# Row gathers of a graph kernel: their indices copied four at a time, 24 tiles ahead, in place of halves of twelve

## The reference, cut to what matters

```
X      = einsum('ne,ref->rnf', out, weights[l])         # 9 edge types, 3 layers l
msg    = X[edge_type, src] + biases[l][edge_type]       # one row per edge
hidden = segment_sum(msg, dst)                          # relu between the layers
x      = layernorm(x + out)
...                                                     # then an attention over the same edges
x      = layernorm(x + attention(x))
```

## Time and profile before

| | |
|---|---|
| median of 3 runs | 4747.55 us (4741.61 to 4761.0) |
| the profiled execution | 4800.08 us, of which the span is 4798.3 us |
| PE busy, DVE busy, POOL busy | 3249.5 us (68%), 3108.2 us (65%), 2833.3 us (59%) |
| layer 0, from its first gather to its last sum | 616 to 1936 us |
| layer 1 | 1993 to 3117 us |
| layer 2, turns with cells | 3173 to 3626 us |
| layer 2, turns without | 3626 to 4257 us |
| attention and output | 4257 to 4798 us |

### The profile page before, as it was taken

How to read it: one execution, slowest core, us unless ns; L and a number is a source line. 1 busy time by engine, 2 the same in 40 slices (tenths; PEclk the granted TensorE clock), 3 DMA queues, 4 the chain that set the end, 5 groups by cost and what they waited for, 6 DMA issues and landing times.

```text
span 4798.3 us, 78742 instructions
## 1 busy us (share of the span) xinstructions
PE 3249.5 (68%) x13288; PEld 1889.5 (39%) x13289; DVE 3108.2 (65%) x9948; ACT 412.4 (9%) x713; POOL 2833.3 (59%) x2838
## 2 busy tenths in 40 slices
PE   7799745556555555766666666676665555669998
PEld 4333223334333333434444444444444444435333
DVE  9999865555555555666666666675664333356998
ACT  2000001000010000001010100101000000000332
POOL 0777866666656566277777777647777777720000
PEclk9899888877878888888889888897895555569998
DMA  5000014433343345645354363565344212134232
GB/s 156 20 0 0 0 45 71 64 58 62 58 65 69 58 61 60 159 67 81 68 76 72 70 78 66 72 155 81 67 65 88 53 53 53 52 54 144 107 133 81
DMA packets 391663, 341.02 MB, mean 71 GB/s; under 512 B 252658, under 2 KB 342314, under 8 KB 388104
## 3 DMA queue, kind: packets, MB, share of 16 engines
q0 software_dynamic: 90368, 165.49, 16.3%
q10 hardware_dynamic: 199392, 60.71, 13.0%
q1 hardware_dynamic: 101672, 112.75, 7.3%
HBM read 231.62 MB, written 107.13 MB: 71 GB/s over the span
## 4 chain that ended last, share of the span: by engine, by line
PE 30%; issue 21%; POOL 17%; DVE 15%; DVEq 9%; DMA 6%; ACT 2%; POOLq 0%; SPq 0%; ACTq 0%
PE ps L876 12%; POOL region L776 8%; POOL scattered_edges L758 8%; PE ps L867 6%; DVE region L510 5%; DVEq L270 5%; DMA region<-x_of_type,idx 5%; PE ps L928 4%; PE ps L910 3%; DVE region L451 3%; PE ps L936 3%; DVE oh L441 2%; PE ps L886 2%; DVEq L510 1%; DVEq L441 1%
## 5 line engine op out<-in xcount | busy, mean ns | idle before, releaser
L776 POOL DMA_INDIRECT region<-x_of_type,idx x2520 | 2435.4, 966 | 1202.3 <-issue 844.0
L876 PE MATMUL ps<-region 128*128 128x510 bf16 x4200 | 1488.7, 435 | 981.6 <-DVE region L451 805.8
L867 PE MATMUL ps<-oh,region 128*128 128x102 f32 x5040 | 1220.5, 334 | 458.4 <-DMA region<-x_of_type,idx 292.1
L867 PEld LDWEIGHTS ps<-oh,region 128*128 128x128 f32 x5040 | 1111.0, 240 | 1007.2 <-issue 333.0
L510 DVE TENSOR_TENSOR region<-region,ps 128x102 f32 x2520 | 657.9, 261 | 1159.3 <-PE ps L867 692.9
L876 PEld LDWEIGHTS ps<-region 128*128 128x128 bf16 x4200 | 451.9, 117 | 1177.9 <-issue 1152.1
L441 DVE TENSOR_SCALAR oh<-iota_w,arrays 128x102 f32<-128x102 f32 x2524 | 630.7, 294 | 162.1 <-issue 141.4
L450 DVE TENSOR_SCALAR region<-iota_w,arrays 128x640 bf16<-128x640 f32 x841 | 471.7, 561 | 221.9 <-PE ps L876 124.7
L758 POOL DMA_INDIRECT scattered_edges<-region x304 | 394.1, 1296 | 208.3 <-DVE ends L385 110.6
L846 PE MATMUL ps<-region 128*128 128x420 f16 x2016 | 410.3, 344 | 25.6 <-DVE region L415 25.6
L451 DVE TENSOR_SCALAR region<-iota_w,arrays 128x510 bf16<-128x510 f32 x841 | 416.7, 496 | 0.0
(11 more groups left out here) (176 smaller groups left out, 1527.8 us busy)
## 6 DMA issues: line engine op xcount, KB each, us to landing
region<-x_of_type,idx POOLq DMA_INDIRECT x2520
edge_counts<-region ACTq DMA_DIRECT2D x31, 1275.0 KB
region<-edge_counts SPq DMA_DIRECT2D x25, 1568.0 KB, 6.5
x_of_type<-region SPq DMA_DIRECT2D x50, 576.0 KB, 5.6
edge_absent<-region ACTq DMA_DIRECT2D x31, 637.5 KB
region<-edge_absent SPq DMA_DIRECT2D x25, 784.0 KB, 4.3
x_of_type<-x0st SPq DMA_DIRECT2D x51, 192.0 KB, 2.0
scattered_edges<-region POOLq DMA_INDIRECT x304
```

The source lines that it names most:

```text
L776: pool.indirect_dma_start(out=grow[:, u % GR, :], out_offset=None, in_=xt, in_offset=bass.IndirectOffsetOnAxis(ap=idx[:, u % GR:u % GR + 1 ...
L867: pe.matmul(ps[:, 6 + n % 2, t * RB:(t + 1) * RB], grow[:, u % GR, :], oh[:, u % U, 0:RB], start=True, stop=True).then_inc(s_used, 1)
L876: mm = pe.matmul(ps[:, c, 0:CW], cl[:, q % 2, c * P:(c + 1) * P], cr[:, q % 2, :], start=False, stop=False, skip_group_check=True)
```

## The change

`put_idx` copies four columns, those of the group of four tiles that has just been summed, and stands behind each of the six groups of the body. Ahead of the loops it is called six times in place of two. GpSimd waits for `s_idx` in front of each group of four and no longer for `s_used`: the copy comes behind the group's sums on VectorE, which come behind its matmuls.

```diff
-    HALVES = GR // 2
-    PUTS = {-(-HALVES * n // SLOTS) - 1: n + 1 for n in range(1, BODY // HALVES + 1)}
...
-            def put_idx(t, h):
-
-                nc_.tensor_copy(idx[:, h * HALVES:(h + 1) * HALVES],
-                                gix[:, bass.ds(t, HALVES)]).then_inc(s_idx, 1)
+            def put_idx(t, n):
+
+                nc_.tensor_copy(idx[:, n * SLOTS:(n + 1) * SLOTS], gix[:, bass.ds(t, SLOTS)]).then_inc(s_idx, 1)
...
-            put_idx(0, 0)
-            put_idx(HALVES, 1)
+            for n in range(GR // SLOTS):
+                put_idx(n * SLOTS, n)
...
-                    if n in PUTS:
-                        put_idx(i * BODY + PUTS[n] * HALVES, PUTS[n] % 2)
+                    put_idx(i * BODY + (GR + n * SLOTS), n)
...
                     for u in range(BODY):
-                        if u % HALVES == 0:
-                            reg_wait(pool, s_idx, i * (BODY // HALVES) + ((NT * l + u) // HALVES + 1))
                         if u % SLOTS == 0:
-                            reg_wait(pool, s_used, i * BODY + (NT * l + u + SLOTS))
+                            reg_wait(pool, s_idx, i * (BODY // SLOTS) + ((NT * l + u) // SLOTS + 1))
```

More of the change, by code:

```diff
@@ L78, in gnn_program @@
     assert CP <= REST and EP % U == 0 and U == 2 * KR and HW <= 512 and NT <= 1 << DIGIT
-    assert BODY == GR and GR % U == 0 and BODY % U == 0 and U == 2 * SLOTS and ET <= KW and NT // HALVES % 2 == 0
+    assert BODY == GR and GR % U == 0 and BODY % U == 0 and U == 2 * SLOTS and ET <= KW
     assert R * NP < 1 << ROW_BIT and RB <= P and ROW_BIT + 7 <= 2 * DIGIT and NB % JB == 0 and PAD_ROW <= NP
```

## The result

The kernel after takes 4819.26 us (4817.85 to 4823.78, 4 runs), the kernel before beside it 4752.32 us: a ratio of 1.0144, 95% interval 1.012 to 1.0168. The forecast was 4742 us with a range up to 4785. The profiled execution of after has a span of 4817.4 us, only 19 us more than that of before; the two medians differ by 67. Before's profile had also begun layer 0 late, at 616.6 us, where after's begins at 605.0 and the later profiles of the kernel before at 605 to 607; so the three layers by themselves have grown by 33 us. The experiments come back to that.

The account below looks back on a forecast made before the run. Layer 0 was taken as slowed by instruction fetches, layer 1 bound by VectorE and TensorE, layer 2's end by GpSimd. Terms 34 + 1 - 12 - 28 + 0 = -5 us on 4747.5 gave 4742 us, range 4700 to 4785.

Parts of the forecast that it names:

- Copies, +34 us: Layers 0 and 1: four more VectorE copies a turn cost 0.12 us each over 70 turns, +34 us; hidden in layer 2.
- The second rival: Layers 0 and 1, behind groups 0, 1, 3 and 4: copies cost 0.24 us each, +28 us, 4776 us; chance 0.20.
- the ring: Layers 0 and 1: TensorE waits for VectorE's L451, VectorE for TensorE's L867; a delay there was said to count once.
- GpSimd's waits, -12 us: Layer 2, turns with cells: GpSimd's waits for copies fall to the 0.30 us any gather shows, -12 us.
- Late gathers, -28 us: Layers 0 and 1: eight tiles more lead remove nearly all TensorE's waits for gathers delayed by ScalarE's stores, -28 us.
- The stall at the head, 0 between -17 and +17 us: Head of layer 0's turns: the body moves four places, still lies in four pieces, and the instruction-fetch stall stays; 0 us.
- an earlier start of the fetch at the turn's end: Layer 0's turns: roughly cancels the 0.3 us of four instructions moved behind the second fetch.
- The sum: Whole kernel: 34 + 1 - 12 - 28 + 0 = -5 us, giving 4742 us.
- I take the difference over as it is: The -5 us, worked out on a profiled execution of 4800.08 us, is applied unchanged to the runs' median of 4747.5 us.
- the copies are hidden: Rival: VectorE's waits before the sums take in the copies, leaving -39 us, 4708 us; chance 0.17.
- the deeper queue brings nothing: Rival: late gathers still stop TensorE and stops use up 24 tiles, +35 us, 4783 us; chance 0.06.
- The last rival: One more instruction ahead of the loop puts layer 0's body in three pieces, removing the stall: -200 - 5, 4542 us; chance 0.07.

Follow-up runs that it names:

- copies with the old waits at place 0: Kernel after with GpSimd's waits of before, layer 0's body at the start of a piece of 128 instructions: 4606.72 us, ratio 0.9612 to the kernel before.
- the kernel before at place 0: Kernel before with five tiny fills ahead of the first loop, so layer 0's body begins a piece of 128 instructions: 4587.91 us, ratio 0.9565 to the unchanged one.
- the ratios 1.0141 and 1.0048: Against the kernel before: kernel after with GpSimd's waits of before, 1.0141; kernel before with four tiny fills ahead of the first loop, 1.0048.
- place 127: Layer 0's body begins on the last place of its piece of 128 instructions: kernel before with four tiny fills, ratio 1.0048; kernel after unchanged, 1.0088.

## Why the prediction was wrong, point by point

**Copies, +34 us.** Size off, and dependent on what stands around them. The undisturbed turn of layer 1 grew by 0.4 us for four of them, near the 0.48 that was read. Without the stall the whole price is about 22 us (copies with the old waits at place 0, against the kernel before at place 0): 15 in layers 0 and 1, where 34 were put, and 5 in layer 2, where nothing was. What hides the rest was not tried. With the stall it is about 44 us by the ratios 1.0141 and 1.0048, of which the profiled stages show 25 in layer 0 and 7 in layer 1. The second rival (the copies cost double) came near for layer 0: 25 us on 34 turns of 4 copies are 0.18 us each, between the forecast 0.12 and its 0.24, and in two of the four places some 0.28. Its reason, a delay paid twice in the ring, was not shown.

**GpSimd's waits, -12 us.** Right: in after's profile all waits above 0.3 us are gone from layer 2 once it has begun, and the layer gained 13 to 18 us in every pair of kernels that differ in them. (The working puts GpSimd's busy share at 0.71 to 0.74 everywhere; in layer 0 it is 814.24 of 1320 us, 0.62. No term hangs on it.)

**Late gathers, -28 us.** The mechanism was right, the size only in part. No wait of TensorE for a gather is left after the first turns. Yet layers 0 and 1 gained 14 us by the new waits without the stall, and with it 8 in layer 1 and nothing in layer 0: there TensorE's waits for late gathers went from 14 us to none, and its waits for L448 rose from 473 to 492.

**The stall at the head, 0 between -17 and +17 us.** This is the step that failed: "an earlier start of the fetch at the turn's end" didn't come, and the four instructions behind the second fetch were not cancelled by anything. They were priced at 0.3 us, 10 us in 34 turns; the heads measured +16, and the end of the turn, where the gain was to be, +8. Alone the move measured +24 us by the ratio, +30 in the profiled stage. That the body would still lie in four pieces, and the counts of 171 and 2 packets, were right. Beside the stall the copies cost more than without it: by ratios 0.93% against 0.47%, and 0.48% for the place. This is a second step that failed: the sum adds the two terms as if neither hung on the other.

**The sum.** 24 for the place, 44 for the copies and -25 for the new waits make +43 us against -5; each is a difference of two ratios along one path from before to after, so the sum must come to the 44 that after showed. The other 23 us of the first comparison are not explained. "I take the difference over as it is" rests on a median of 4747.5 us that the experiments don't repeat: beside them this kernel took 4776 to 4808 us in every run on four chips, near the first profile's 4800. The 4752 us are 0.8% below those chips, and after's 4819 only 0.3% below its 4836; why is open, since no profile of the kernel before at 4752 us was taken.

**The other rivals.** That the copies are hidden (4708 us) and that the deeper queue brings nothing (4783 us) are both ruled out: copies alone cost 22 us without the stall and 44 with it, and the queue alone gained 45 and 25. **The last rival** (chance 0.07) was right in mechanism and price and missed by one instruction: -208 us for the kernel before, where it had -200.

## What to carry to other kernels

Before pricing an edit inside a hardware loop, count instructions: where a body reached into a fourth piece of 128 instructions, as here, each turn paid for fetches, and one to five dummy instructions ahead of the loop were worth ten times the edit that was being discussed (208 us against 21). Measure an edit at a fixed place of the body, or its own effect drowns: this one gains 21 us where both kernels are free of the stall, loses about 19 where both have their body at place 127 (1.0088 against 1.0048), and loses 44 as it stands, where it also moves the body. And try few, wide copies for a deeper queue: three of eight columns kept GpSimd as free of waits in layer 2 as six of four, and took 23 us less.

## What the runs showed of the hardware

VectorE's instruction stream comes in pieces of 128 instructions (8.2 KB a packet). A loop whose body lies in three pieces runs without fetches (2 packets in 1000 us); one in four pieces fetches five a turn (171 in 34 turns), presumably its four and the one behind them, and from the last copy of a turn to the next first L450 5.3 to 5.7 us pass. Beside other transfers it is longer: in the kernel before, the head at 1295 us, from the last sum to the first L450, took 5.5 us with the DMA engines at a share of 0.21, and the one at 1334 us took 17.6 us at 1.13. The border was hit exactly: bodies of 274 to 282 instructions at places 111, 123 and 127 stall, at place 0 they do not. The Trainium skill, page "Runtime: NRT & Kernel Launch", section "Instruction fetch mechanics", describes the same stall for a taken branch out of the held window; the sizes that it gives, blocks of 256 instructions and two of them, are not what these runs show, packets of 128 and fetches only once a body lies in four of them, and the measurement decides.

A copy of 0.20 us on GpSimd between indirect DMAs, with the wait for its end, costs 0.64 us of its pace (1.89 us for 1.25). And chips differ: the kernel before took 4789 to 4795 us on four of them and 6580 us on a fifth; the 4752 us of the first comparison are on record without their chip.
